# Single score products in attention, a joined last block in the shared experts, sooner expert loads and router scores in four column quarters

## What is computed

```python
q = (layernorm(x) @ w_q.T).reshape(B, S, 8, 4, 16)
k, v = ctx @ w_k.T, ctx @ w_v.T            # 8 groups of width 16
attn = softmax(causal(q @ k.T / 4))        # a key mask too
x = x + tanh(g1) * ((attn @ v) @ w_o.T + b_o)
xt = layernorm(x)                          # 2048 tokens
scores = softmax(xt @ Wg.T)                # 16 experts
combine = top 4 of scores, inside the 2 best of 4 groups
y = sum over e of combine[e] * ((silu(xt @ W1[e].T) * (xt @ W3[e].T)) @ W2[e].T)
z = (silu(xt @ Ws1.T) * (xt @ Ws3.T)) @ Ws2.T
x = x + tanh(g2) * (y + z)
```

## Time and profile before

| | us |
|---|---|
| median of 3 runs | 1355.91 (1350.62 to 1359.08) |
| the profiled execution, its own time | 1353.09 |
| its span, first to last instruction | 1351.3 |
| PE busy / weight loads | 1272.3 / 936.9 |
| DVE, ACT, POOL busy | 646.7, 586.4, 642.8 |
| granted TensorE clock, mean | 0.979 of 2.4 GHz |

### The profile page before, as it was taken

How to read it: one execution, slowest core, us unless ns; L and a number is a source line. 1 busy time by engine, 2 the same in 40 slices (tenths; PEclk the granted TensorE clock), 3 DMA queues, 4 the chain that set the end, 5 groups by cost and what they waited for, 6 DMA issues and landing times. The chain is left out here.

```text
span 1351.3 us, 27369 instructions
## 1 busy us (share of the span) xinstructions
PE 1272.3 (94%) x8553; PEld 936.9 (69%) x8554; DVE 646.7 (48%) x1861; ACT 586.4 (43%) x1016; POOL 642.8 (48%) x722
## 2 busy tenths in 40 slices
PE   8998999999997998999999799999999999999995
PEld 5554544444443357778767589999989988889894
DVE  4345788888896654686304113232343333333300
ACT  1222566666663223222222145555545444445452
POOL 6000333333332431443455266666666666666664
PEclk8999999999998997999999899999999999999998
DMA  9452333333343404000013225555555554665433
GB/s 338 150 162 89 111 109 100 97 107 99 95 126 120 159 1 187 32 32 32 32 55 103 96 52 139 141 142 142 137 132 141 142 139 129 157 174 129 91 71 39
DMA packets 73615, 152.94 MB, mean 113 GB/s; under 512 B 10725, under 2 KB 16357, under 8 KB 72793
## 3 DMA queue, kind: packets, MB, share of 16 engines
q1 hardware_dynamic: 52104, 100.27, 22.1%
q0 software_dynamic: 21456, 51.97, 18.4%
HBM read 97.56 MB, written 52.23 MB: 111 GB/s over the span
## 5 line engine op out<-in xcount | busy, mean ns | idle before, releaser
L202 DVE CUSTOM_DVE_ANT_0 a_mb<-a_mb,late 128x128 f32<-128x128 f32 (+3 forms) x512 | 244.4, 510 | 50.8 <-PE a_mb L183 44.1
L1439 DVE CAST e_w<-e_w 128x480 fp32r<-128x480 f32 x135 | 75.5, 568 | 360.4 <-DMA e_w<-in_w2T 360.4
L634 ACT ACTIVATE a_at<-a_eb 128x1024 f32<-128x1024 f32 (+3 forms) x256 | 179.6, 705 | 102.4 <-PE a_eb L696 101.8
L570 POOL TENSOR_SCALAR_AFFINE_SELECT a_at<-a_at 128x256 f32<-128x256 f32 x256 | 105.5, 412 | 225.4 <-ACT a_at L634 225.2
L1593 PE MATMUL e_yps<-e_w,e_hT 128*128 x711 | 197.3, 404 | 0.9 <-ACT e_hT L1504 0.9
L1572 PE MATMUL e_gate<-e_w,e_xT 128*128 x948 | 169.8, 328 | 8.5 <-DVE e_w L1448 7.8
L1572 PEld LDWEIGHTS e_gate<-e_w,e_xT 128*128 128x128 f32 x948 | 156.7, 190 | 20.7 <-issue 16.4
L1572 PE MATMUL e_up<-e_w,e_xT 128*128 x948 | 170.6, 329 | 0.0
L1572 PEld LDWEIGHTS e_up<-e_w,e_xT 128*128 128x128 f32 x948 | 149.8, 188 | 0.0
L1593 PEld LDWEIGHTS e_yps<-e_w,e_hT 128*128 128x128 f32 x711 | 128.1, 189 | 25.5 <-issue 1.2
L1470 POOL TENSOR_TENSOR e_hT<-e_hc,e_hT 128x384 fp32r<-128x384 f32 x79 | 84.3, 1067 | 118.9 <-ACT e_hc L1505 118.9
(11 more groups left out here) (235 smaller groups left out, 1844.5 us busy)
## 6 DMA issues: line engine op xcount, KB each, us to landing
e_w<-in_w13T SPq DMA_DIRECT2D x16, 1408.0 KB
dq<-p_parts SPq DMA_DIRECT2D x32, 256.0 KB, 2.4
a_q<-dq SPq DMA_DIRECT2D x64, 128.0 KB
do<-a_o SPq DMA_DIRECT2D x32, 256.0 KB, 2.1
e_w<-in_w2T SPq DMA_DIRECT2D x16, 512.0 KB
a_k<-dk SPq DMA_DIRECT2D x64, 98.0 KB
e_w<-in_ctxT SPq DMA_DIRECT2D x4, 1024.0 KB, 13.9
e_w<-in_x SPq DMA_DIRECT2D x4, 1024.0 KB, 13.2
```

Source lines behind the costliest of these rows:

```text
L202: eng.tensor_tensor_reduce(out=b[:, 0:w], in0=b[:, 0:w], in1=io["late"][:, SEQ - w:SEQ], scale=1.0, scalar=3 * NEG, op0=ALU.add, op1=ALU.m ...
L570: eng.affine_select(out=square, in_=square, compare_op=ALU.is_ge, fill=0.0, base=0, pattern=[[0, 2], [1, P]], channel_multiplier=-1).then_ ...
L634: eng.activation(at[r % 2][:, ch, 2 * hp:2 * hp + 2, ch * P:SEQ], eb[hp][:, :, ch * P:SEQ], ACT.Exp, scale=0.25).then_inc(s_exp, 1)
```

## The change

Five edits. (1) In attend, the products for maxima are issued singly: the odd one ahead of the pair for the exponentials, the next even one behind it and ahead of the value products; that of the next item's first is at the end of this item. Each waits only for its own bank (`free`); of each 18 bank places two are left out, the 5th and the 14th, so that two products in each half of the item use the bank of the product two before instead of three before. The transposed maxima go into an unused corner of `a_eb`, and ScalarE copies them (L209's work leaves VectorE). (2) In close, the router's scores of the batches 0 to 2 are made with the router's matrix as weights, four products of 512 columns in the four column quarters of the array, then copied by ScalarE and summed and turned by four products against a 0/1 matrix; batch 3 keeps the old form. (3) In shared, the last 64 gate rows and the last 64 up rows are one block of 128, so the sixth block has 12 products instead of 24. (4) The very last tile's result is scaled and added by VectorE in one instruction, and the load of expert 1's weights is issued in the next block. (5) In experts, the load of w1/w3 waits only for the last up product of the expert that had the buffer, the load of w2 for its last down product as before.

```diff
-SKIPPED, TURNED = HG, HG + 1
+OPS = [(t, j, ch) for pair in PAIRS for j in range(2) for t, ch in pair]
+NOPS = len(OPS)
+SLOTS = [m + (m >= NOPS // 4) + (m >= 3 * NOPS // 4) for m in range(NOPS)]
+PERIOD = NOPS + 2
...
+def bank(io, m):
+    return io["mb"][SLOTS[m] % RING]
+def free(m):
+    slot = SLOTS[m] - RING
+    while slot % PERIOD not in SLOTS:
+        slot -= RING
+    return SLOTS.index(slot % PERIOD) + slot // PERIOD * NOPS + 1
+def find_maxima(eng, io, i, r, m):
+    t, j, ch = OPS[m]
+    if not isinstance(i, int) or i * NOPS + free(m) > 0:
+        eng.wait_ge(io["s_rmax"], i * NOPS + free(m) + 1)
+    rows, w = slice(HALF * t, HALF * t + ROW_MAX), max(256, (ch + 1) * P)
+    eng.matmul(bank(io, m)[:, 0:w], ...)
...
+        turned = eb[0][0:HG * CH, 1, 0:P]
+            def take_row(i, r, t):       # on ScalarE
+                eng.wait_ge(io["s_mt"], i + 3)
+                eng.activation(io["mrow"][(r + 1) % 2], turned, ACT.Copy).then_inc(s_mr, 1)
...
-            def exp_unit(i, r, ch, j):
+            def exp_unit(i, r, ch, j, order):
+                if ch == 1 and j == 0 and exists(i + 1):
+                    turn_maxima(eng, io, turned, r + 1, (i + AHEAD) * NOPS + 1)
...
                 for ch in range(CH):
                     for j in range(2):
+                        m = 2 * (2 * ch + j) + 1
                         if exists(i + AHEAD):
-                            max_pair(eng, io, i + AHEAD, (r + AHEAD) % NB, ch, j)
-                        exp_unit(i, r, ch, j)
+                            find_maxima(eng, io, i + AHEAD, (r + AHEAD) % NB, m)
+                        exp_unit(i, r, ch, j, (1 - OPS[m][0], OPS[m][0]))
+                        if m + 1 < NOPS and exists(i + AHEAD):
+                            find_maxima(eng, io, i + AHEAD, (r + AHEAD) % NB, m + 1)
+                        elif m + 1 == NOPS and exists(i + AHEAD + 1):
+                            first_maxima(i + AHEAD + 1, ...)
                         pv_units(i, r, 2 * ch + j)
...
+            def score_chunks(b):
+                for k in range(KD):
+                    mm = eng.matmul(tp[1][32 * k:32 * k + 32].rearrange("p k n -> p (k n)"), wide[:, k, :], x2T[b][:, k, :],
+                                    start=True, stop=True, tile_position=(0, 32 * k))
+                mm.then_inc(s_part, 1)
+            def add_chunks(b):
+                eng.wait_ge(s_taken, b + 2)
+                for j in range(CH):
+                    mm = eng.matmul(lp[:, j, :], turned[:, j * P:(j + 1) * P], sums4[:], start=True, stop=True)
...
-                if i > LAG:
-                    score(*divmod(i - LAG - 1, CH))
+                b, j = divmod(i - LAG - 1, CH)
+                if j == CH - 1 and 0 <= b < BATCH - 1:
+                    score_chunks(b)
+                if j == 0 and 1 <= b < BATCH:
+                    add_chunks(b - 1)
+                if i > NT + LAG - CH + 1:
+                    score(BATCH - 1, i - (NT + LAG - CH + 2))
...
                 if i >= 2:
                     eng.wait_ge(s_act, i)
+                    eng.wait_ge(s_upc, i)
                 multiply(i, n, 0, gate, s_gate)
-                multiply(i, n, 1, up, s_up)
+                if n < NS - 1:
+                    multiply(i, n, 1, up, s_up)
...
+            eng.wait_ge(s_down, NT + 1)          # VectorE, last tile
+            eng.scalar_tensor_tensor(out=last, in0=yps[(NT - 1) % 2][:], scalar=tg[:, 0:1], in1=last,
+                                     op0=ALU.mult, op1=ALU.add).then_inc(s_v, 1)
...
-            eng.wait_ge(s_down, NT + 1)
-            eng.wait_ge(io["s_base"], 16 * NT)
-            load_expert(eng, io, 1, 1)
...
+            eng.wait_ge(io["s_base"], 16 * NT)   # SP, block of the experts
+            load_first(eng, io, 1, 1)
+            load_second(eng, io, 1, 1)
...
+                    eng.wait_ge(s_up, free)
+                    load_first(eng, io, u * 2 + r, r)
                     eng.wait_ge(s_down, free)
-                    load_expert(eng, io, u * 2 + r, r)
+                    load_second(eng, io, u * 2 + r, r)
```

186 lines of the change are left out of this document (104 added, 82 removed).

## The result

The median of the changed kernel is **1509.33 us** (1503.53 to 1523.87, 4 runs) against 1354.45 (1350.62 to 1359.08, 4 runs): a ratio of **1.1156**, 95% interval 1.1082 to 1.1229. The forecast was 1331, and the range ended at 1345.

What follows compares the result with a forecast made beforehand. In attend TensorE and VectorE hold each other up; elsewhere TensorE works nearly without a gap. Terms -1 + 0.5 - 3.5 - 6.4 - 4.4 - 1 - 7.8 = -23.6 from the 1355.91 median gave 1331, range 1308 to 1345.

Steps and rivals of the forecast that it cites:

- attend at -1 us: Attend: finer waits give back at even products nearly all they save at odd ones; -1 us over 28 items.
- the rival that ended slower, even products that block: Attend: banks free 0.15 us later, five slots in eight lose it; +21 us, up to 1369 in all; chance 0.04.
- The walk of an item: Attend: the new order followed through one item with prices from the rows; 9.18 us an item against 9.22.
- Its two waits: Attend: products 4 and 12 wait for their banks with value products queued behind, 0.48 us each.
- The transposition's new place: Attend, between two groups of 64-row products: nothing new by the rows, at most 0.13 us an item or 4 us.
- the row's move to ScalarE: Attend: ScalarE's copy, about 0.3 us, is hidden in its idle time; +0.5 in all allowed for the last two items.
- Close: Close: router scores in column quarters save TensorE work, partly lost to waits for ScalarE; -3.5, from 0 to -6.
- Shared: Shared: the joined block saves products, but TensorE then waits 1.55 us for the low part; -6.4 over four batches.
- batch 1: Shared: here the routing table's products stand between and cover the wait for the low part, leaving a gain of 2.8.
- The meeting: Meeting of all engines after shared: VectorE's single scale-and-add lets TensorE start sooner, 2.7 us idle instead of 7.15; -4.4.
- the -1: Behind the meeting after shared: with less idle time the clock may stay up; -1, from 0 to -2.5.
- the seven waits: Experts: TensorE's waits for split expert weights, 7.8 us in all, go with the earlier load; -7.8, from -6 to -8.

Runs made afterwards that it cites:

- before_no_fill: The kernel before without the 24 bf16 products ahead of each exp pair of the first item: 1476.97 us, ratio 1.0911.
- row_only: Changed kernel, attend keeping only the moved row (transposition in `a_eb`, ScalarE's copy), with maxima products paired behind a joint wait as before: 1359.14 us, ratio 1.0051.
- gap_split: no_attend with each piece's low half, in VectorE's split of expert weights, made right behind its high half: 1329.45 us, ratio 0.9825.
- late_load: no_attend with both loads of expert weights behind the last down product, as before: 1342.08 us, ratio 0.9914.
- attend_only: The kernel before with edit (1) alone, including its part in the projection stage: 1493.17 us, ratio 1.1046.
- two_more: Changed kernel with two bf16 products added ahead of each exp pair of every item but the first: 1688.69 us, ratio 1.2474.
- no_attend: Changed kernel without edit (1), the attend stage and its part in the projection stage as before: 1367.10 us, ratio 1.0109.

## Why the prediction was wrong

**Attend: the step that failed is the clock.** The prediction put attend at -1 us; it measured +143.1. It took the full clock of the earlier trace rows as given for the new order, and asked after the clock only in close and at the meeting. before_no_fill shows what it stood on: 24 x 8 bf16 products in the first item, and the old order, which keeps what they raise. No rival had this; the rival that ended slower, even products that block, had the right place and the wrong mechanism (+1.3 us an item for 1369; measured +0.39, and 143 us through the clock).

**The walk of an item was off by 0.44 us** (9.18, measured 9.62). Its two waits were nearly right: the products 4 and 12 start 0.70 and 0.79 us behind their slots (169.83 to 170.53, 175.00 to 175.79), where product 2, which waits for nothing, starts 0.34 behind (168.81 to 169.15); so they wait 0.36 and 0.45 for the 0.48 of the walk. Mis-sized was TensorE's own work around the transposition. The value products of slot 3 were to start 3.34 us into the item, at the pace of ScalarE's chain, and start at 3.67 (168.81 to 172.48): ahead of them stand the odd product, the transposition, the exponentials and the even product one behind another, 1.06 us from 171.42. That is 0.33 of the 0.44. At the half clock, where VectorE is no limit, the order's own price is bare: 14.73 against 13.54.

**The transposition's new place** was to cost nothing by the rows, and at most 0.13 us an item by a difference in them, 0.41 less 0.28. That difference was misread: it is a wait for VectorE, whose reduction ahead of the next product ended at 253.32, 0.05 ahead of its start. From the kernel before:

```profile
253.18 0.14 DVE L202 DVE_READ_ACCUMULATOR2_ANT a_mx<- 128x1 f32 x1
```

So the row says nothing of the rule that the prediction set beside it, and no run here tests that rule alone. What the new place costs is in row_only's rows, 0.16 us an item or 5 us, where the row's move to ScalarE had been put at +0.5 in all. (Two figures beside it were off as well and changed nothing in the sum: VectorE's work for an item adds up to 7.5 us by the terms given, not 7.7, and w1/w3 are 1408 of 2112 KB, 67% and not 73%.)

**Close** was -3.5. In gap_split it is -2.5 from the first `c_den` to its end (102.8 to 100.3), of which 0.5 goes in a longer meeting. The quarters were right (1.07), the waits for ScalarE behind them were 1.10 and 0.81 instead of 0.8 for both. A wait of 0.91 for VectorE's `c_o` ahead of a projection is new and was at nothing in the sum (491.20 in gap_split, 0.12 before).

**Shared** was -6.4; gap_split has -4.0 (228.5 to 224.5). The waits came, 1.26, 1.41 and 1.41 us in three batches, near the 1.55, and these batches gave 1.24, 1.23 and 1.24 us, as forecast. The step that failed is batch 1: the routing table was to cover its wait and leave 2.8 us, and the batch gave 0.55, because the table's own products now come too soon for VectorE's `r_atcol` and wait 1.66 us, where before none of them waited. From gap_split:

```profile
624.97 1.34 PE L1382 MATMUL r_tokps<-r_atcol,e_x 128*128 128x158 f32 x8 [1.66 <-DVE r_atcol L1218]
```

In the changed kernel and in late_load the clock also fell for 3.4 us behind a wait of 1.85 in batch 3; there shared gave only 1.4 and 0.8.

**The meeting** was -4.4 and measured -4.5. The clock didn't stay up behind it (in gap_split it is back at 1.00 8.6 us behind TensorE's start, before 6.7), so the -1 did not come.

**Experts.** That the seven waits would go was right. The step "What is late next is nothing: the split is 12 us of VectorE that is otherwise idle" was wrong: idle on VectorE is not idle for GpSimd. With the gap the term is -11.0, more than the -7.8: TensorE's waits in the stage go from 12.0 us to 3.3, the seven and one of 1.2 for GpSimd among them, and the last 2.1 us are not accounted for.

So the other four edits, with one order changed, give nearly what was forecast for them: their terms add up to 23.1 us, and gap_split (1329.45) is 21.3 under the kernel before on its own chip (1350.70). That its time stands just under the 1331 is luck of two kinds. Errors offset each other: shared, close and the clock's 1 us were forecast too high by 4.9 together, the experts too low by 3.2. And the kernel before ran 5 us faster there than the 1355.91 that the forecast started from.

## What to carry to other kernels

A clock at 1.00 in a long stage is a thing to account for: look at what raised it (here 192 short bf16 products in the first item) and cost an edit that makes a period longer, here by 4%, with the whole stage at half speed as its rival. When work for VectorE moves in time, look at what GpSimd does in the new place as well, and put a dependent pair of operations next to each other where VectorE runs a long chain beside GpSimd. Count two products in opposite row groups as one: parted, the second cost TensorE another 0.32 us here. When work is taken away from one engine, look at every engine that used to be just in time, as VectorE's `r_atcol` was.

## What the hardware showed that I had not expected

TensorE at 99 to 100% busy can stay at 1.2 GHz for 389, 440 and 608 us (attend_only and the changed kernel, before_no_fill, two_more). Sixteen short products put between row groups cost 5.4 us an item. A GpSimd subtraction of 1.0 us took up to 6.6 us beside a chain of casts and subtractions on VectorE, and 1.0 to 1.5 when the chain was reordered so that a gap of 0.04 us stood in it. What decides without gaps which of both gives way was not settled: two splits that began at the same point of GpSimd's scatter, 1.15 and 1.14 us behind its start (changed kernel and no_attend), went one the one way and one the other.
